# In two pairs of a batch the value sum stands between the two score groups, and the next pair's keys behind them

## What is computed

```
xn = layernorm(ctx); ln = layernorm(layernorm(x))
q  = ln @ Wq * 64**-0.5                      # 16 heads of 64
k, v = split(concat(xn, ln) @ Wkv)           # 512 keys
sim  = where(mask, q @ k.T, -max)            # 256 x 512 per head
out  = softmax(sim) @ v                      # the value sum
x    = x + tanh(g) * layernorm(out @ Wout)
```

## Time and profile before

| | us |
|---|---|
| timed runs, median of 3 | 4344.7 (4343.72 to 4346.62) |
| profiled execution | 4317.87 |
| its span | 4316.1 |
| TensorE busy in the span | 3976.5 (92%) |
| VectorE, ScalarE, GpSimd busy | 2323.2 (54%), 1772.2 (41%), 945.7 (22%) |

### The profile page before, as it was taken

One profiled execution on the slowest core, in us unless ns is written; L12 is line 12 of the kernel. 1 busy time (PEld: TensorE's weight loads), 2 busy tenths in 40 slices (PEclk: granted clock), 3 DMA queues, 4 the chain that ended last, 5 costly groups with the idle time before them and its releaser, 6 DMA issues. The chain is left out here.

```text
span 4316.1 us, 78135 instructions
## 1 busy us (share of the span) xinstructions
PE 3976.5 (92%) x29168; PEld 2824.2 (65%) x29168; DVE 2323.2 (54%) x7158; ACT 1772.2 (41%) x3733; POOL 945.7 (22%) x1118
## 2 busy tenths in 40 slices
PE   7999999999999999999998899988999998769996
PEld 4666666666666666666665589966666666438963
DVE  4555655565556655665554522125566666474445
ACT  4455555555555455545542211113444444313420
POOL 2221222122212221222120011111000000005667
PEclk9999999999999999999999999999999999879998
DMA  3000000000000000000000169940000100029964
GB/s 114 1 4 9 8 6 4 9 8 6 3 9 8 6 4 9 8 6 4 6 13 33 74 237 333 332 165 13 30 23 26 31 21 11 13 71 299 335 200 143
DMA packets 136623, 284.25 MB, mean 66 GB/s; under 512 B 19968, under 2 KB 90176, under 8 KB 127680
## 3 DMA queue, kind: packets, MB, share of 16 engines
q1 hardware_dynamic: 84944, 200.03, 13.3%
q0 software_dynamic: 18336, 50.09, 4.0%
q10 hardware_dynamic: 32976, 29.13, 2.0%
HBM read 229.12 MB, written 50.07 MB: 65 GB/s over the span
## 5 line engine op out<-in xcount | busy, mean ns | idle before, releaser
L466 POOL TENSOR_SCALAR a_wide_p<-a_wide_p,a_w_inv 128x512 f32<-128x512 f32 x512 | 355.3, 706 | 1438.8 <-DVE a_w_inv L1133 1438.8
L903 ACT ACTIVATE a_wide_p<-a_wide_p,a_row_min 128x512 f32<-128x512 f32 x512 | 363.4, 713 | 114.0 <-DVE a_row_min L1128 112.5
L1203 DVE TENSOR_REDUCE a_q_pad<-ring 128x4 f32<-128x1024 f32 x256 | 301.1, 1219 | 87.5 <-PE ring L696 87.4
L1128 DVE CUSTOM_DVE_ANT_0 a_wide_p<-ring,a_neg_keys 128x512 f32<-128x512 f32 x403 | 266.0, 688 | 125.0 <-PE ring L550 124.8
L550 PE MATMUL ring<-a_qk 64*128 64x512 f32 x806 | 289.1, 643 | 21.6 <-DVE a_row_min L1128 15.0
L960 ACT ACTIVATE a_probs<-ring 128x1024 f32<-128x1024 f32 x256 | 250.5, 1019 | 72.6 <-PE ring L710 72.6
L1621 PE MATMUL ring<-b_xgt,b_we 128*128 128x128 f32 x2016 | 235.7, 275 | 0.5 <-DVE b_xgt L1784 0.5
L1621 PEld LDWEIGHTS ring<-b_xgt,b_we 128*128 128x128 f32 x2016 | 230.2, 192 | 1.1 <-DVE b_xgt L1784 0.7
L2689 DVE CUSTOM_DVE_ANT_0 c_junk<-ring,c_neg_mask 128x256 f32<-128x256 f32 x512 | 181.4, 420 | 89.3 <-PE ring L2219 89.3
L529 PE MATMUL acc<-a_kv_t,shared_w 128*128 128x512 f32 x392 | 196.0, 623 | 1.2 <-ACT a_kv_t L894 1.2
L1550 POOL DMA_INDIRECT d_xg<-d_rows,d_token_idx x159 | 150.1, 944 | 178.6 <-PE ring L1610 102.3
(11 more groups left out here) (464 smaller groups left out, 8547.3 us busy)
## 6 DMA issues: line engine op xcount, KB each, us to landing
b_we<-in_experts SPq DMA_DIRECT2D x63, 1536.0 KB, 9.3
d_we<-in_experts SPq DMA_DIRECT2D x159, 256.0 KB, 4.6
d_results<-d_yb ACTq DMA_DIRECT2D x159, 128.0 KB
b_results<-b_yb ACTq DMA_DIRECT2D x63, 128.0 KB, 9.0
a_cb<-in_ctx SPq DMA_DIRECT2D x16, 256.0 KB, 2.8
b_turned<-a_heads_t SPq DMA_DIRECT2D x16, 256.0 KB
b_rows<-a_heads SPq DMA_DIRECT2D x16, 256.0 KB
shared_x<-b_turned SPq DMA_DIRECT2D x8, 512.0 KB, 5.7
```

The lines of the kernel that those rows point to most:

```text
L466: ins = pool.tensor_scalar(wide_p[:, h % 4, t, :], wide_p[:, h % 4, t, :], w_inv[:, t, h:h + 1], 1.0, ALU.mult, ALU.mult)
L903: ins = act.activation(wide_p[:, h % 4, t, :], wide_p[:, h % 4, t, :], ACT.Exp, scale=-1.0, bias=row_min[:, h, t:t + 1], accum_out=row_sum ...
L1128: dve.tensor_tensor_reduce(wide_p[:, h % 4, t, :], wbank(name), neg_keys[w % 2][:], -0.125, 3.0e38, ALU.add, ALU.min, row_min[:, h, t:t + ...
L1203: dve.tensor_reduce(q_pad[:, :, 2 * i:2 * i + 2, HD].rearrange("p t h -> p h t"), s, AX.X, ALU.max, negate=True).then_inc(nr.taken(name), 1)
```

## The change

In pairs 2 and 6 (`between`) AV of the previous pair is issued between the two score groups, and K of the next pair behind the second group (in pair 2 behind place 11, in pair 6 behind place 31), directly ahead of Q. The order list, TensorE's program and ScalarE's program are changed alike; VectorE, GpSimd and SyncE are not. On ScalarE the copy of AV moves ahead of the exponentials of the first group and the copy of K from there to behind those of the second group and what `beside` holds at the place.

```diff
--- before.py
+++ after.py
@@ -304,6 +304,7 @@
 
                 late = (0, 1, 5)
                 near = (1, 2, 5, 6)
+                between = (2, 6)
 
                 w_order = []
                 for i in range(-1, B + 2):
@@ -311,11 +312,12 @@
                         nw, nu = pair_after(i, u)
                         bw, bu = pair_before(i, u)
                         w_order += [("S", i, u, 0, j) for j in range(2)] * on(i)
-                        w_order += [("K", nw, nu)] * (u not in late and on(nw)) + filled(i, 5 * u)
+                        w_order += [("AV", bw, bu)] * (u in between and on(bw))
+                        w_order += [("K", nw, nu)] * (u not in late + between and on(nw)) + filled(i, 5 * u)
                         w_order += [("S", i, u, 1, j) for j in range(2)] * on(i)
-                        w_order += [("AV", bw, bu)] * (u in near and on(bw))
+                        w_order += [("AV", bw, bu)] * (u in near and u not in between and on(bw))
                         w_order += ([("wo", i - 1)] * (u == 1 and on(i - 1)) + filled(i, 5 * u + 1)) * (u in near)
-                        w_order += [("K", nw, nu)] * (u in late and on(nw)) + [("Q", nw, nu)] * on(nw)
+                        w_order += [("K", nw, nu)] * (u in late + between and on(nw)) + [("Q", nw, nu)] * on(nw)
                         w_order += filled(i, 5 * u + 1) * (u not in near)
                         w_order += ([("lT", i + 1)] * (u == 6 and on(i + 1)) + filled(i, 5 * u + 2)) * (u in near)
                         w_order += [("V", i, u)] * on(i)
@@ -839,14 +841,16 @@
                                     scores(i, u, 0)
                                 if u == 0 and on(i - 2):
                                     by_query("c", i - 2, 3)
-                                if u not in late and on(nw):
+                                if u in between and on(bw):
+                                    pair_values(bw, bu)
+                                if u not in late + between and on(nw):
                                     keys(nw, nu)
                                 beside(i, 5 * u)
                                 shared(i, 5 * u)
                                 if on(i):
                                     scores(i, u, 1)
                                 if u in near:
-                                    if on(bw):
+                                    if u not in between and on(bw):
                                         pair_values(bw, bu)
                                     beside(i, 5 * u + 1)
                                     shared(i, 5 * u + 1)
@@ -854,7 +858,7 @@
                                     by_query("f", i - 1, 3)
                                 if u == PAIRS - 1 and on(i - 1):
                                     by_query("c", i - 1, 0)
-                                if u in late and on(nw):
+                                if u in late + between and on(nw):
                                     keys(nw, nu)
                                 if on(nw):
                                     pair_queries(nw, nu)
@@ -1051,7 +1057,7 @@
                                 if u in near:
                                     if u != 2 and on(i):
                                         exps(i, u, 1)
-                                    if u > 1 and on(bw):
+                                    if u > 1 and u not in between and on(bw):
                                         pair_values(bw, bu)
                                     beside(i, 5 * u + 1)
                                     if u == 1 and on(bw):
```

## The result

The changed kernel takes 4333.1 us (median of 20 runs, 4325.6 to 4344.0), the kernel before, measured beside it, 4341.1 (20 runs, 4330.5 to 4346.6): ratio 0.9984, 95% interval 0.9977 to 0.9992. So it is faster, by 0.16%, less than the 0.2% that I set as the border of "no change". Forecast were 2.6 us; measured are about 7, between 3.5 and 10 (the medians lie 8.0 apart). Part of that is the starting point: the three runs that the forecast started from had a median of 4344.7, the twenty have 4341.1.

The account below looks back on a forecast made before the run. TensorE, busy for 96% of phase A, was taken to bound the kernel. The terms summed to 15 x (-0.27 + 0.00) + 1.4 = -2.6 us, from 4344.7 to 4342.1 us; range 4336.5 to 4347.6.

Parts of the forecast that it names:

- TensorE sets the pace, and a change of tile shape costs 0.09 to 0.10 on either side: Phase A: TensorE 96% busy; a full-shaped step pays 0.10 after another shape, 0.09 before one.
- Pair 2, 8.88: Batches 1 to 15, first scores to V: 9.15 us before, 8.88 after, so 0.27 saved per batch.
- my upper bound: Pair 2: 0.35 saved per batch if fq also falls to K's full-shape length, 1.72.
- Batch 0, +1.44: Pair 2 of batch 0: V at 54.67 waits for K's bank, free at 56.11; 1.44 us lost once.
- The 1.3 of cover: Pair 2, batches 1 to 15: K copied by about 1024.5, V, said to wait for that bank, at 1025.8.
- Pair 6, 0.00: Batches 1 to 15: nothing saved, as gate logits now follow AV's shape; between +0.10 cost and 0.10 gain.
- 0.4 worked out: Pair 6: K taken by 1097.15 at the latest, V starts at 1097.53; the thinnest cover in the change.
- The starting point: Median of the timed runs, 4344.7 us, 26.8 above the profiled execution; carried over into the forecast.
- (a): Rival: order on TensorE doesn't matter, nothing saved, batch 0 costs 1.4: 4346.1 us; chance 0.15.
- (c): Rival: more than forecast, pairs 3 and 7 lose a wait too: 4334.8 us; chance 0.12.
- (b): Rival: K's late copy on ScalarE holds V, 1.4 per batch, 4363 us; chance 0.07, small form (4345) 0.04.

Follow-up runs that it names:

- phase A alone: Kernels cut off behind phase A, phases B to D left out, with one store of x: kernel before 2470.2 us, changed kernel 2465.1 us.
- a_klate: Kernel before, phases B to D left out; in pair 2 K goes behind the second score group, nothing between the groups: 2482.5 us.
- a_both: Kernel before, phases B to D left out; in pair 2 AV goes between the score groups and K stays there too: 2474.5 us.
- a_klast: Changed kernel, phases B to D left out; in pair 6 of batches 1 to 15 ScalarE copies K behind Q and c's turned keys: 2484.3 us.
- a_after: Changed kernel cut off behind phase A (phases B to D left out), against the kernel before cut off alike: 2465.1 us against 2470.2.
- a_before: Kernel before, cut off behind phase A with one store of x (phases B to D left out): 2470.2 us.
- a_wider: Against a_gate, pair 5 too has AV between its score groups: 2466.7 us against 2460.2.
- a_gate: Changed kernel, phases B to D left out; pair 6's gate logits go behind the second score group, gate exponentials behind K's copy: 2460.2 us.

## Why the prediction was wrong

Its range missed the time, and its effect was too small: 2.6 us, where phase A alone gained 5.05 and the whole kernel about 7. The step that failed is the loss of 1.44 us in batch 0. What bounds the kernel, the sign and the pair that gains were right. That the time lies outside the range comes from the starting point as well: from 4344.7, even phase A's 5.05 would have ended inside it.

- **TensorE sets the pace, and a change of tile shape costs 0.09 to 0.10 on either side: right.** K 1.91 and 1.72 came as read, AV 1.88 ahead of scores, 9.74 measured for 9.72 worked out in `a_klate`. The Trainium skill ("TensorE: Matmul & The Clock Gate", Part 2, LDWEIGHTS) gives a weight load as its columns over 1.2 GHz, an estimate of 107 ns for 128 columns. One load for one change fewer is too little for the 0.19 by which K fell; but K lost another shape on both of its sides, and two loads would be 0.21. These runs show neither which count is right nor that weight loads are the cause; the measured 0.19 decides.
- **Pair 2, 8.88: mis-sized by 0.08.** It is 8.80, because fq too fell to full-shape length once x_t was early. That was my upper bound and should have been the value: fq's 1.80 was read where x_t came only just before it; where it had to wait for x_t (`a_both`) it is 1.80 as well, and with x_t early (changed kernel, `a_klate`) 1.72. 15 x 0.08 = 1.2 us.
- **Batch 0, +1.44: the step that failed.** The prediction said "V waits for that bank". In pair 2 it does not. Nothing stands between Q and V there, so counting three back from V gives the second bank of the scores, and it is the first turn of the weights that takes K's bank. I had counted as in pair 6, where the turn lT stands between (in the code it turns the context and not, as the prediction has it, the latents; nothing hangs on that). TensorE and ScalarE in batch 0 of the changed kernel:
```profile
54.73 1.03 PE L540 MATMUL ring<-a_kv_t,shared_x 128*128 128x256 f32 x4
55.60 1.95 PE L560 MATMUL ring<-shared_w,a_kv_t 128*128 128x128 f32 x16
57.38 0.60 PE L570 MATMUL acc<-ident,a_wide_p 128*128 128x128 f32 x4
```
```profile
55.82 0.58 ACT L914 ACTIVATE a_qk<-acc 128x512 f32<-128x512 f32 x1
```
V started before K's copy did, and the turn at 57.38 had no need to wait. The 1.4 us of forecast loss did not come; pair 2 of batch 0 even became shorter, from its scores to those of pair 3 11.56 us and not 11.72. The 1.3 of cover that the prediction gave to V in pair 2 of the other batches is for the same wrong bank; nothing hung on it. Put right, the sum is 15 x (-0.35) = -5.2, with the 0.16 of batch 0 some -5.4; phase A alone measured -5.05.
- **Pair 6, 0.00: right**, and by the reason given: the gate logits pay what K no longer pays. K's copy ended in time, with about 0.5 of cover (0.4 worked out); `a_klast` shows what lies beyond.
- **The starting point.** 4344.7 rested on three runs; the later median is 3.6 lower. My range had room for the costs and none for that. With -5.2 and 4341.1 the forecast would have been 4335.9. So of the 9.0 us between 4342.1 and 4333.1, 3.6 are the starting point and 2.6 the effect; 2.8 stay open. They lie inside the interval of the measured gain (3.5 to 10).
- **Rivals.** (a), that the order does not matter, fell with `a_after` and `a_both`. (c), waits lost in pairs 3 and 7, did not happen: from 300 to 2200 us TensorE waits for other engines in the same seven groups before and after, each within 0.7 us of its sum before. In (b) the mechanism is real and was half a microsecond away, but its 1.4 per batch stood on batch 0's wait, which isn't there.

## What to carry to other kernels

Where one engine of many small products sets the pace, read each step's length in its surroundings: K between two steps of another tile shape was 0.19 us (11%) dearer than among its like, and swapping it with a step that has another shape anyway paid this back without an instruction less. A swap in a rotation of buffers has to be counted out place by place for each variant of the order, because who waits for whom three places on changes with what stands between. And a gain of some microseconds was found by leaving out the stages that did not change: the spread fell from 18 us to 2.

## What the runs showed of the hardware

In batch 1 TensorE stands idle for 2.7 us, and behind that its granted clock can be at the lower level of 1.2 GHz (0.50) for a while whose length is not the program's. Windows of the kernel before (columns as in the earlier trace rows, the clock is the third from the end):
```profile
150.00:153.00 3.00, 3.00 (x6) 0.84 (x3) 1.77 (x6) 0.00 (x0) 0.00 (x0) 0.50 0.00 0
153.00:156.00 3.00, 3.00 (x7) 0.84 (x5) 0.19 (x1) 1.03 (x2) 0.00 (x0) 0.57 0.00 0
```
and of `a_before`, with the same instructions in the same order up to there:
```profile
150.00:153.00 3.00, 3.00 (x6) 0.83 (x3) 1.53 (x5) 0.00 (x0) 0.00 (x0) 0.50 0.00 0
153.00:156.00 3.00, 3.00 (x15) 1.04 (x15) 0.98 (x3) 1.71 (x4) 0.00 (x0) 0.98 0.03 8
```
The first batch's way was 145.89 us in the one and 144.46 in the other. In `a_wider`, idle there for 2.71 us as well, the clock did not fall at all:
```profile
150.00:153.00 3.00, 3.00 (x22) 1.36 (x20) 1.96 (x6) 0.76 (x2) 0.00 (x0) 1.00 0.02 5
```
and its first batch was 1.47 us shorter than its later ones, where that of the kernel before was 1.57 longer. So of the 1.7 us that the changed kernel's profile gained in the first batch (144.20), only some 0.35, the gain of every batch, can be put down to the change.

A step made only of weight loads also has a price for the step behind it. While the gate logits run in `a_gate` (1087.24 to 1088.15), TensorE loads weights in all of the 0.91 us, and K directly behind takes 1.80 and not 1.72, though both have full shape; that is where most of the missing half of the expected 0.20 stayed.
